# Layers 0, 5 and 7 of an eight-layer gated block: expert outputs summed per expert in PSUM and added to x with the token's weight as a per-partition scalar, router in pieces between the tiles

## What is computed

```python
# layer 0: four experts, the token's id picks one; layer 5: two experts of width 1024, the router's best one
# layer 7: eight experts of width 128, the best two with normalised weights, and a shared one of width 512
probs = softmax(x @ w_gate)                     # layers 5 and 7 (layer 0: one-hot of the token id)
h_e   = silu(x @ gate_e) * (x @ up_e)           # layer 0 has one product, used for both
out   = sum_e weight[token, e] * (h_e @ down_e)
```

## Time and profile before

| | us |
|---|---|
| median of 3 runs | 1732.45 |
| lowest, highest | 1725.73, 1734.65 |
| the profiled execution's own time | 1730.8 |
| its span in the profile | 1728.8 |
| layer 0: first gate matmul to first add to x | 20.4 to 84.8 |
| layer 5: last xt_lo to first add to x | 1422.1 to 1571.1 |
| layer 7: last xt_lo to end of the last add to x | 1614.8 to 1724.4 |

### The profile page before, as it was taken

The page is one execution under the profiler, slowest core; times in us unless marked ns, Lnnn a source line. Parts: engine busy times, 40 slices in busy tenths (PEclk is TensorE's granted clock), DMA queues, the critical chain, the costliest instruction groups (busy, mean ns, idle before and its releaser), DMA issues.

```text
span 1728.8 us, 31404 instructions
## 1 busy us (share of the span) xinstructions
PE 1468.2 (85%) x11544; PEld 865.2 (50%) x11544; DVE 1345.9 (78%) x2321; ACT 752.7 (44%) x1439; POOL 927.5 (54%) x861
## 2 busy tenths in 40 slices
PE   4868999999769998789999997478788878994698
PEld 2544555555423232646565655255555564652354
DVE  6767877787679998857878776778888857789675
ACT  3432222222258897322222223578788842221222
POOL 4435667666110140026766660899999963763162
PEclk9989999999855555789999998555555568997899
DMA  5120111111049999101111111578888831111010
GB/s 193 37 68 28 47 53 45 45 47 53 10 75 179 177 177 184 59 10 55 45 45 45 55 43 31 97 141 141 138 137 143 144 82 43 46 46 37 10 37 25
DMA packets 325534, 132.92 MB, mean 77 GB/s; under 512 B 308145, under 2 KB 308657, under 8 KB 324529
## 3 DMA queue, kind: packets, MB, share of 16 engines
q1 hardware_dynamic: 323840, 125.54, 35.0%
q10 hardware_dynamic: 1584, 5.92, 1.0%
HBM read 54.87 MB, written 1.05 MB: 32 GB/s over the span
## 4 chain that ended last, share of the span: by engine, by line
PE 56%; DVE 23%; POOL 13%; issue 3%; ACT 2%; DMA 1%; SPq 0%; POOLq 0%; DVEq 0%; ACTq 0%
PE s_all L686 40%; PE bank L686 8%; DVE small L1572 7%; POOL c_hi L606 4%; POOL c_lo L606 3%; PE s_all L770 3%; DVE xn L1317 2%; POOL c_hi L604 2%; POOL c_lo L604 2%; PE s_all L895 1%; DVE stats L1306 1%; DVE small L1575 1%; DVE ffbuf L1437 1%; PE s_all L696 1%; DVE ffbuf L1431 1%
## 5 line engine op out<-in xcount | busy, mean ns | idle before, releaser
L1439 DVE TENSOR_TENSOR hid_lo<-ffbuf,hid_hi 128x512 f16<-128x512 f32 x224 | 383.3, 1711 | 155.8 <-ACT hid_hi L1112 155.8
L478 POOL TENSOR_TENSOR w_hi<-w_in,ws_col 128x768 f16<-128x768 f32 (+1 forms) x112 | 160.9, 1437 | 534.7 <-PE bank L686 519.1
L1112 ACT ACTIVATE hid_hi<-ffbuf 128x512 f16<-128x512 f32 x224 | 141.0, 630 | 672.1 <-DVE ffbuf L1437 672.1
L686 PE MATMUL s_all<-xt_hi,w_hi 128*128 128x512 f16 x864 | 262.1, 386 | 26.2 <-DVE ffbuf L1437 23.3
L479 POOL TENSOR_SCALAR w_in<-w_in 128x768 f32<-128x768 f32 (+1 forms) x112 | 274.7, 2453 | 0.0
L686 PE MATMUL s_all<-xt_lo,w_hi 128*128 128x512 f16 x864 | 262.1, 386 | 0.0
L686 PE MATMUL s_all<-xt_hi,w_lo 128*128 128x512 f16 x864 | 261.8, 385 | 0.0
L1437 DVE TENSOR_TENSOR ffbuf<-ffbuf,s_all 128x512 f32<-128x512 f32 x224 | 154.1, 688 | 72.0 <-PE s_all L770 24.5
L482 POOL TENSOR_TENSOR w_lo<-w_in,w_hi 128x768 f16<-128x768 f32 (+1 forms) x112 | 185.0, 1652 | 9.4
L1572 DVE TENSOR_REDUCE small<-s_all 128x1 f32<-128x1024 f32 x128 | 155.5, 1215 | 12.7 <-PE s_all L895 12.7
L1177 ACT ACTIVATE ag<-s_all,small 128x1024 int16<-128x1024 f32 x128 | 154.1, 1204 | 19.1 <-DVE small L1575 9.4
(11 more groups left out here) (306 smaller groups left out, 2755.0 us busy)
## 6 DMA issues: line engine op xcount, KB each, us to landing
w_in<-in_w_blocks SPq DMA_DIRECT2D x112, 384.0 KB, 3.0
region<-in_w_attn SPq DMA_DIRECT2D x4, 512.0 KB, 11.3
sel<-in_k_sel ACTq DMA_DIRECT2D x1, 1280.0 KB, 5.8
sel<-in_k_sel ACTq DMA_DIRECT2D x1, 1152.0 KB, 5.5
ag<-ag SPq DMA_TRANSPOSE x66, 3.3
x<-in_x_in SPq DMA_DIRECT2D x1, 1024.0 KB, 6.0
region<-in_ctxt SPq DMA_DIRECT2D x1, 1024.0 KB, 9.7
ffbuf<-in_mask ACTq DMA_DIRECT2D x1, 1024.0 KB, 4.8
```

The lines of the kernel that those rows point to most:

```text
L478: nc.gpsimd.tensor_tensor(hi, w, ws_col[:, 0:1].broadcast_to([P, used]), ALU.mult).then_inc(s_g, 1)
L686: m = nc.tensor.matmul(outp, lhs, rhs, start=(first and n == 0), stop=(last and n == len(steps) - 1), skip_group_check=True)
L1112: nc.scalar.activation(hid_hi[:, h, :], hid[:, h, :], ACT.Copy).then_inc(s_hh, 1)
L1439: nc.vector.tensor_tensor(hid_lo[:, h, :], hid[:, h, :], hid_hi[:, h, :], ALU.subtract).then_inc(s_hl, 1)
```

## The change

Layers 0, 5 and 7 leave `combine`, `cwt`, the weight transposes, the zero matmuls and the selector load out. Their `down` starts a new PSUM sum at each expert's first block, and at an expert's last block `take` on DVE adds banks 4 to 7 to x, per 128-token tile, times the weight of the token as a per-partition scalar (L1591, 128x256). Layer 0 has four experts of two blocks, layer 5 two of eight, layer 7 eight of one block and the shared one of four, which keeps the 128x512 form (L1597). Layer scales that sat in the weights move into them or into L1575. PE's order becomes `gate_up(n+1)`, `down(n-1)`; the router's matmuls come after the first `gate_up` and write banks 6 and 7. DVE's router is cut in three parts, after the products of halves 0, 1 and 2; the id router of layer 0 comes after the product of half 0. The context rounding in layer 5 moves one half later. All halves of the three layers are written out, without hardware loops.

```diff
+SELECTED = [1, 3]
+EXPERTS = {0: [2] * 4, 5: [8] * 2, 7: [1] * 8 + [4]}
+ROUTED = {0: 4, 5: 2, 7: 8}
...
 # PE
+            def ffn_out(l):
+                def gate_up(n):
...
+                    if n > 1:
+                        pe.wait_ge(s_hid, 2 * first + n - 1)
...
+                def down(n):
...
+                    e, fresh, _ = expert_of(l, n // 2)
+                    pe.wait_ge(s_hl, 2 * first + n + 1)
+                    if fresh and e:
+                        pe.wait_ge(s_acc, emptied(l, e - 1, h))
...
+                        m = mm3(bank[4 + i // 2][:, (i % 2) * D:(i % 2 + 1) * D], [pair], first=fresh and i % 2 == 0, last=False)
...
+                gate_up(0)
+                if l in ROUTER:
+                    router(l)
+                gate_up(1)
+                for n in range(1, halves):
+                    if n + 1 < halves:
+                        gate_up(n + 1)
+                    down(n - 1)
+                down(halves - 1)
 # ACT
+                for n in range(halves):
+                    hidden(n)
+                    if n + 1 < halves:
+                        gate(n + 1)
+                    if n == 0 and l in ROUTER:
+                        router(l)
 # DVE
+                def take(e, h):
...
+                    dve.wait_ge(blk_done, 2 * (first + blk) - 1 + h)
...
+                    if e < ROUTED[l]:
+                        for i in range(4 * h, 4 * h + 4):
+                            m = nc.vector.scalar_tensor_tensor(out=x[:, i, :], in0=bank[4 + i // 2][:, (i % 2) * D:(i % 2 + 1) * D],
+                                                               scalar=weights[:, i, e:e + 1], in1=x[:, i, :],
+                                                               op0=ALU.mult, op1=ALU.add)
...
+                for n in range(halves):
+                    hidden(n)
+                    if l in ROUTER and n == 0:
+                        router(l, 1)
+                    if l in ROUTER and n in (1, 2):
+                        router(l, n + 1)
+                    if l == 0 and n == 0:
+                        id_router()
+                    e, _, ends = expert_of(l, n // 2 - 1) if n > 1 else (0, False, False)
+                    if ends:
+                        take(e, n % 2)
+                    hidden_low(n)
```

More of the change, by code:

```diff
@@ L365, in n_whole, with expert_of, emptied @@
             return k // HPG
+        def expert_of(l, blk):
+            done = 0
+            for e, n in enumerate(EXPERTS[l]):
+                if blk < done + n:
+                    return e, blk == done, blk == done + n - 1
+                done += n
+        def emptied(l, e, h):
+            earlier = sum(len(EXPERTS[m]) for m in EXPERTS if m < l)
+            return 2 * (earlier + e) + h + 1
+        SKIPPED = 2 * FFN[1][0]
         FIRST_LOADS, LOADS = 4, 10
@@ L1342, in id_router, with router @@
                 link(nc.vector.tensor_copy(weights[:, :, 3], id_ge[:, 2, :]))
-            def router(l):
+            def router(l, part):
                 n = list(ROUTER).index(l)
@@ L1360, in router @@
                     link(nc.vector.tensor_scalar(o2n_map, iota, o2n_f, None, ALU.is_equal))
[L1361 to L1367, removed]
+                if part == 1:
+                    dve.wait_ge(s_logit, n + 1)
+                    for b in range(2):
+                        m = nc.vector.tensor_scalar(logits[:, 4 * b:4 * b + 4, 0:ne],
+                                                    bank[b0 + b][:, :].rearrange("p (t e) -> p t e", t=4)[:, :, 0:ne],
+                                                    XW, None, ALU.mult)
+                    link(m)
+                    if l in EXPERTS:
+                        nc.vector.memset(scratch[:, 0:1], 0.0).then_inc(s_lgr, 1)
+                if part == 1 and l == 3:
                     for i in range(NT):
@@ L1384, in router @@
[L1384 to L1392, removed]
@@ new lines, in router @@
+                if part == 2:
+                    dve.wait_ge(s_rexp_in, n + 1)
+                    if top < 8:
+                        link(nc.vector.memset(top8[:, :, top:8], BIG))
+                    for i in range(NT):
+                        m = nc.vector.match_replace(replaced[:, i, 0:pad + 8], top8[:, i, :], logits[:, i, 0:pad + 8],
+                                                    -BIG / 2)
+                    link(m)
+                    link(nc.vector.tensor_tensor(replaced[:, :, 0:ne], replaced[:, :, 0:ne], logits[:, :, 0:ne],
+                                                 ALU.not_equal))
@@ L1400, in router @@
+                if part == 3 and l == 1:
                     pair = weights[:, :, 0:32].rearrange("p t (c g) -> p t c g", g=2)
```

220 lines of the change are left out of this document (146 added, 74 removed).

## The result

The changed kernel takes 1687.89 us (median of 4 runs, 1686.27 to 1692.67) against 1730.87 (4 runs, 1725.73 to 1734.65): ratio 0.9759, 95% interval 0.9741 to 0.9778. The forecast was 1696.6, from a median before of 1732.45 over three of these four runs; the time lies 2.1 us under the low end of the forecast's own range, 1690, and 0.1 us under that of the wider one, 1688. The gain by medians, 43.0 us, is 7 more than the sum of 35.8. Direction and the main mechanism were right, and the gain was put too low, mostly in layer 0. Its profiled execution took 1686.27 (span 1684.5), so the traces differ by 44.3 us in span, and that is what I divide up here.

A forecast was written before the change was run, and what follows sets the result against it. It took PE to bound layer 7, DVE layer 0, and DVE's context parts to stall PE in layer 5. Gains of 9.6 + 18.5 + 7.7 = 35.8 us gave 1696.6 us, own range 1690 to 1703, wider range 1688 to 1712.

The forecast's parts named there:

- Layer 7, steps: Layer 7, gate_up(2) to gate_up(23): 21 steps each lose combine's 0.22 us of PE, 4.6 us gained.
- DVE fits with nothing to spare: Layer 7 routed blocks: DVE with POOL's turns needs 7.9 us against PE's 7.80; 0.8 us charged for eight blocks.
- the first rival: DVE becomes layer 7's bound: hid_lo meets POOL in every half, 4.48 us a half, 1705.7 us; chance 0.17.
- Layer 7, start: Layer 7: gate_up(0) starts at xt_lo, before the router, so gate_up(2) comes at 1623.8 instead of 1627.06, 3.3 us earlier.
- The stall: Layer 5: PE waiting for DVE's four context parts lost 9.7 us; 8.0 would be saved and 1.7 stay.
- put product 1 at 30.6 instead of 34.49: Layer 0 start: product, id router, hid_lo and context maximum after SiLU(0) bring product 1 3.9 us earlier.
- now run at PE's pace: Layer 0's last eight halves: 2.60 us each, say 21.0 us instead of 23.6, 2.6 gained.
- the next norm meets them as before: After layer 0: POOL's four splits for layer 1 meet the next norm unchanged, so no gain or loss.
- the selector loads ... lie off the path: Selector loads of layers 5 and 7, like the loops' register instructions, count for nothing in the sum.
- that rival: ACT's table switches drain, 2.66 us each: down(2) waits 2.3 us in each of layers 5 and 7, 1701.2 us; chance 0.05.
- the last two rivals: Layers 5 and 7 straight-line code slower, 1724.6 us, chance 0.04; layer 7 waits drop PE's clock, 1759, chance 0.03.
- The stall in layer 5: Rival: a product is late at gate_up(9) and PE's clock falls again, 8.0 us less gain, 1704.6 us; chance 0.10.

The follow-up runs named there:

- the second profile: The unchanged changed kernel run and profiled once more: median 1689.19 us, ratio 0.9753; layer 0 69.42 us with its first gate_up at half speed.
- the nine: The nine profiles of kernels that share the changed kernel's layer 0 and 1 code: layers 0 and 1 together take 440.9 to 446.8 us, mean 443.4.

## Why the prediction was right, and where its terms were off

- **Layer 7, steps: right.** 7.80 us per two halves, 21 steps of 0.22, no L770. Charged 0.8 us for turns with POOL: wrong. "DVE fits with nothing to spare" let hid_lo meet POOL's third operation; in the trace the take is what stands there, and it isn't held up. DVE idles 0.37 and 0.96 us per block, and a fifth add costs next to nothing. With it falls the first rival, DVE as the bound.
- **Layer 7, start: mechanism right, 5.85 us instead of 3.3.** The failed step is "at 0.43 us a matmul ... it takes 5.2 us": I moved the half speed of before along with gate_up. It took 2.6. About 2 us of this gain hang on a clock that had risen in seven profiles of nine, which I had not foreseen. The order itself is worth 1.4 us then, and the rest is what was removed.
- **Layer 7, end:** 7.15 us from gate_up(23) (21 steps of 3.90 after 1589.57, 1671.47) to the last add at 1678.62, forecast 6.9. Before it was 9.5, so the end gave 2.3.
- **Layer 5: 17.8 against 18.5, by errors that cancel.** The start gave 4.25 us, not 3.3 (gate_up(0) took 4.2 us where 5.2 was charged). The stall gave 6.2 by the traces and 5.2 to 5.9 by the runs that leave the parts out, not 8.0; its residue, 1.7 forecast, was 1.7 of PE idle and 2.2 by experiment. The end gave 2.9, not 1.4: "gate_up(31) near 1563.6" is a misreading, it starts at 1562.06, so the end before was 9.0 us and not 7.5. Not foreseen were 1.4 us of layer 6's xn beside POOL's last split. That the sum came within 0.7 us is luck.
- **Layer 0: 13.9 against 7.7 (12 to 13 over all profiles), the term that failed.** The failed steps are "put product 1 at 30.6 instead of 34.49", "now run at PE's pace" and "the next norm meets them as before". Product 1 came at 28.13 (28.31 in the second profile): "the selector loads ... lie off the path" held for layers 5 and 7, but layer 0's ran beside x's load, and xn began 1.1 us earlier without it (with layer 0 put back it starts at 10.55, and at 9.67 to 9.86 in the nine; that it is the load and nothing else of layer 0's code isn't separated); the last xt_lo ended 0.5 and 1.1 us earlier, and the id router took 2.6 and 2.15 us, not 3.15. The next seven halves gave 3.0, as forecast. The last eight took 19.9 us, not 21.0, since DVE is never idle before a product there: its own 1.99 us (no take) and 2.76 (with a take) per half count, not PE's 2.61. The 1.2 us charged for turns did not come, and layer 1's xn gave 1.5, where "the next norm meets them as before" had nothing. Part of this is chance: xn took 7.8 to 8.1 us in the three profiles with the combine form, and 6.2 to 6.3 in six and 8.8 in three of the changed one, 7.1 in the mean.
- **The table switches cost nothing.** ACT timeline, layer 7:

```profile
1590.38 1.28 ACT L1163 ACT_TABLE_LOAD   x1
...
1591.68 0.26 ACT L1163 ACTIVATE region<-region 128x64 f32<-128x64 f32 x1
...
1592.47 1.28 ACT L1205 ACT_TABLE_LOAD   x1
...
1593.77 0.60 ACT L1205 ACTIVATE ffbuf<-s_all 128x512 f32<-128x512 f32 x1
```

Two loads of 1.28 us, each followed by its activation 0.02 us later, and PE not idle. The drain that the Trainium skill adds (ScalarE: Activation LUTs, What ACT_TABLE_LOAD costs) isn't seen in these rows: the trace disagrees, and that rival falls. Nor did the last two rivals show: straight-line code keeps PE's pace, and PEclk is 1.00 with PE busy throughout in layer 7's stretches. The stall in layer 5 did not stay.

## What to carry to other kernels

When two engines take turns at SBUF, write down for each operation whether all its operands lie in SBUF or one in PSUM: here the adds and products with one operand in PSUM lay over the other engine's long operations and cost their own length only, and they shielded what would have been held up. Ask of a slow stretch at a stage's start whether its slowness belongs to the work or to the clock, before moving it. And read a gain of some microseconds by stages in several profiles: the totals of either kernel vary by 6 to 9 us, while layer 5 repeated within 0.4 and layers 6 and 7 within 0.1 in all profiles with their code, except where the clock came otherwise; layers 0 and 1 did not repeat so well, and there the mean of several profiles is needed.

## What the runs showed of the hardware

- A scalar_tensor_tensor with one operand in PSUM is not held up by POOL: all 112 adds of the takes last 0.47 or 0.48 us each, with POOL at work or not, and a take of four 1.65 to 1.66. That is what lets the takes in for their own length. hid_lo, with two in SBUF, took 1.27 us instead of 0.68 beside POOL's middle operation (1614.65, 2.13 us), yet ended at 1616.02, 0.76 before it. The Trainium skill (SBUF — State Buffer, SBUF: two separate sides) names DVE operations with two SBUF inputs among those that take the shared ports, against a GpSimd operation that reads SBUF, which the trace bears out, and says that the other side is blocked for the whole instruction, which this row does not (POOL's spans in a profile are rough, but 0.76 us is over half of what hid_lo takes).
- xn, whose one tensor operand lies in SBUF, is held up: eight took 2.67 us alone, 4.07 to 8.79 beside POOL's splits.
- The granted clock at a restart is not fixed by the code: with gate_up right behind the transposes it was full in seven profiles and half in two in layer 7; with the router between it was full at first and fell in five of five. The Trainium skill (TensorE: Matmul & The Clock Gate, What's actually happening) says that the point of the rise does not start from the kernel's own work and so varies from run to run; the runs agree. In layer 0 of the second profile the view prints a granted clock of 1.00 throughout, while two matmuls of gate_up(0) took 0.86 us and not 0.43: the trace's first record of the clock is its rise at 23.64, and the view prints 1.00 for the time ahead of it. There the matmuls' own pace tells the clock.
